# Two graph layers on one core: first sums of three chunks put ahead of the next logits, byte comparisons against a number held in PSUM, and destination one-hots moved to ScalarE

## What is computed

```python
def gat_conv(h, src, dst, fc_w, attn_l, attn_r, bias, heads, out_feats):
    feat = (h @ fc_w.T).reshape(n, heads, out_feats)
    el = jnp.sum(feat * attn_l, axis=-1)
    er = jnp.sum(feat * attn_r, axis=-1)
    e = jax.nn.leaky_relu(el[src] + er[dst], 0.2)
    m = jax.ops.segment_max(e, dst, num_segments=n)
    ex = jnp.exp(e - m[dst])
    ssum = jax.ops.segment_sum(ex, dst, num_segments=n)
    a = ex / ssum[dst]
    return jax.ops.segment_sum(feat[src] * a[..., None], dst, num_segments=n) + bias
```

## Time and profile before

| | us |
|---|---|
| median of three runs | 2154.1 |
| the profiled execution | 2160.66 |
| its span, first to last instruction | 2158.5 |
| first sums, gathers on POOL | 78 to 617 |
| second scores, VectorE's one-hots | 698.0 to 836.2 |
| gathers for the second sums, POOL | 693 to 1255 |
| mean granted TensorE clock | 0.80 |

### The profile page before, as it was taken

How to read it: one execution, slowest core, us unless ns; L and a number is a source line. 1 busy time by engine, 2 the same in 40 slices (tenths; PEclk the granted TensorE clock), 3 DMA queues, 4 the chain that set the end, 5 groups by cost and what they waited for, 6 DMA issues and landing times.

```text
span 2158.5 us, 28964 instructions
## 1 busy us (share of the span) xinstructions
PE 1510.8 (70%) x7753; PEld 1147.0 (53%) x7754; DVE 1450.5 (67%) x2290; ACT 419.1 (19%) x780; POOL 1369.4 (63%) x1396
## 2 busy tenths in 40 slices
PE   5345656666777443888566688877778777489997
PEld 3234544544666342676454545655555555368874
DVE  3457787777886786776444465777676666777766
ACT  1100000000004000000000043444444444110127
POOL 0477777777731888777777714677777777135544
PEclk9657877777888555999878788888787877689999
DMA  2654444444414664444434436899999999778811
GB/s 89 168 130 122 126 122 124 125 125 125 120 49 151 174 171 138 135 129 129 120 115 120 123 96 235 299 342 339 339 349 335 343 335 341 281 248 294 292 69 60
DMA packets 234909, 406.15 MB, mean 188 GB/s; under 512 B 33199, under 2 KB 171621, under 8 KB 228197
## 3 DMA queue, kind: packets, MB, share of 16 engines
q0 software_dynamic: 73216, 219.89, 32.7%
q1 hardware_dynamic: 161637, 185.66, 27.3%
HBM read 330.93 MB, written 74.48 MB: 188 GB/s over the span
## 4 chain that ended last, share of the span: by engine, by line
POOL 49%; PE 20%; issue 17%; DMA 7%; DVE 5%; SPq 1%; ACT 1%; ACTq 0%; DVEq 0%; POOLq 0%
POOL row_space L876 45%; PE ps L1190 9%; DMA row_space<-tab_kv,src_i 3%; DMA item_v<-row_space 3%; PE ps L1291 2%; PE ps L1412 2%; POOL base L885 2%; POOL acc L885 1%; PE ps L963 1%; PE ps L991 1%; PE ps L1300 1%; PE ps L1432 1%; POOL arena L885 1%; PE ps L1215 1%; DMA arena<-rows_block_dst 1%
## 5 line engine op out<-in xcount | busy, mean ns | idle before, releaser
L876 POOL DMA_INDIRECT row_space<-tab_feat,src_i x760 | 757.1, 996 | 302.7 <-issue 231.2
L876 POOL DMA_INDIRECT row_space<-tab_kv,src_i x416 | 394.2, 948 | 197.7 <-issue 123.7
L1190 PE MATMUL ps<-arena 128*128 128x257 f32 (+1 forms) x1664 | 422.0, 415 | 121.7 <-DVE arena L2170 115.6
L1190 PEld LDWEIGHTS ps<-arena 128*128 128x128 f32 x1664 | 339.6, 208 | 197.5 <-issue 139.0
L1291 PE MATMUL ps<-arena 128*128 128x265 f32 x768 | 234.8, 470 | 95.9 <-DVE ps L2413 47.3
L1086 PE MATMUL ps<-acc,arena 128*128 x832 | 284.3, 501 | 0.0
L2164 DVE TENSOR_TENSOR arena<-row_space,ps 128x1280 f32<-128x1280 f32 (+1 forms) x94 | 174.3, 1855 | 141.7 <-DMA row_space<-tab_feat,src_i 139.9
L1291 PEld LDWEIGHTS ps<-arena 128*128 128x128 f32 x768 | 177.1, 236 | 142.1 <-issue 102.8
L1582 ACT COPY acc<-ps 128x265 f32<-128x265 f32 (+2 forms) x75 | 28.3, 377 | 1105.6 <-PE ps L1190 545.1
L1982 DVE TENSOR_TENSOR arena<-row_space,ps 128x1024 f32<-128x1024 f32 x104 | 126.8, 1220 | 137.4 <-PE ps L1086 86.2
L1086 PEld LDWEIGHTS ps<-acc,arena 128*128 128x128 f32 x832 | 196.6, 248 | 38.3
(11 more groups left out here) (380 smaller groups left out, 2176.6 us busy)
## 6 DMA issues: line engine op xcount, KB each, us to landing
item_v<-row_space SPq DMA_DIRECT2D x52, 1024.0 KB, 7.9
row_space<-item_v SPq DMA_DIRECT2D x52, 1024.0 KB, 4.9
arena<-rows_block_dst SPq DMA_DIRECT2D x104, 128.0 KB
row_space<-tab_feat,src_i POOLq DMA_INDIRECT x760, 2.8
scores<-rows_block_dst SPq DMA_DIRECT2D x52, 128.0 KB
arena<-rows_src_low SPq DMA_DIRECT2D x52, 128.0 KB
row_space<-tab_kv,src_i POOLq DMA_INDIRECT x416
arena<-rows_type SPq DMA_DIRECT2D x52, 128.0 KB
```

What stands on the lines that cost most here:

```text
L876: nc.gpsimd.indirect_dma_start(rows_of_slot(s)[:, g, :], None, table, bass.IndirectOffsetOnAxis(ap=src_i[:, item:item + 1], axis=0),).then ...
L1190: last = nc.tensor.matmul(ps[:, SUM_BANKS:2 * SUM_BANKS][:, bass.ds(bs[g], 1), 0:width].rearrange("p a d -> p (a d)"), onehot[:, s % 2, g, ...
```

## The change

Three edits.

**First sums, order.** `sums_first` now runs chunks 9, 10 and 11, and `period` only chunks 0 to 8 and 12. Inside `sums_first` the terms of chunk c+2 are spread out: groups 0 and 1 between the builds, 2 and 3 between the steps of the softmax. On PE, register loads move behind `carries`, and each of these chunks has 11 warm products ahead of the shares and 6 behind the factors.

**Comparisons against PSUM.** ScalarE and VectorE write the partition's own number (and, for `hot`, the numbers 0 to 24) into spare columns of PSUM. The byte comparisons of the first sums, the sources' half of those of the second scores, and `hot` read that copy: `tensor_scalar` with a pointer becomes `tensor_tensor` with a broadcast column in PSUM.

**Second scores, destinations.** VectorE compares only the sources' row (1024 bytes instead of 2048). ScalarE makes the destinations' one-hots: Square of (byte - own number) into one of four buffers, then Relu of 1 - square. The broadcasts have four buffers instead of two; the sources' row waits for VectorE's one-hot, the destinations' row for ScalarE's Relu. PE waits for both one-hots.

```diff
+                def spread_both(u, s, first):
+                    for k, made in ((0, onehot_made), (1, dst_onehot_made)):
+                        if not first and k == 0:
+                            sp.wait_ge(made[s % 2], nth(u, s) + HALF)
+                        if not first and k == 1:
+                            sp.wait_ge(made[s % 2], nth(u, s) - 1)
+                        row = flat[k][bass.ds(u * (STEP * P // 2) + s * GROUP * P // 2, GROUP * P // 2)]
+                        sp.dma_start(bcast_words[:, s, k], row.partition_broadcast(P)).then_inc(bcast_in[s], 16)
...
                         pe.wait_ge(onehot_made[s % 2], nth(u, s) + (layer * HALF + 2))
+                        pe.wait_ge(dst_onehot_made[s % 2], nth(u, s) + 1)
...
-            idle("score2")
+            def dst_squares(u, s, first):
+                act.wait_ge(bcast_in[s], u * 32 + (32 + (broadcasts(1) if s < 2 else 0)))
+                if not first:
+                    act.wait_ge(dst_onehot_made[s % 2], nth(u, s) - 1)
+                nc.scalar.activation(dst_square[:, s], bcast[:, s, 1], ACT.Square,
+                                     bias=minus_part_no[:]).then_inc(act_step, 1)
+                step.add()
+            def dst_relu(u, s, still):
+                act.wait_ge(act_step, step.value() - still)
+                act.wait_ge(score_mm[s % 2], nth(u, s) + HALF)
+                nc.scalar.activation(onehot_t[:, s % 2, 1], dst_square[:, s], ACT.Relu, scale=-1.0,
+                                     bias=ones[:, 0:1]).then_inc(dst_onehot_made[s % 2], 1)
...
                 z = s % 2
-                dve.wait_ge(bcast_in[z], nth(u, s) * 32 + (32 + broadcasts(layer)))
-                vec.tensor_scalar(onehot_t[:, z], bcast[:, z], part_no[:], None,
+                dve.wait_ge(bcast_in[s], u * 32 + (32 + (broadcasts(layer) if s < 2 else 0)))
+                own = ps[:, 4 * z:4 * z + 1, NUMBERS_AT + BLOCKS:NUMBERS_AT + BLOCKS + 1].rearrange("p a x -> p (a x)")
+                vec.tensor_tensor(onehot_t[:, z, 0], bcast[:, s, 0], own.broadcast_to([P, GROUP * P]),
                                   ALU.is_equal).then_inc(onehot_made[z], 1)
...
-                    vec.tensor_scalar(dst_onehot[:, z], dst_bytes[:, z], part_no[:], None,
+                    vec.tensor_tensor(dst_onehot[:, z], dst_bytes[:, z], ps[:, SHARE_BANK, OWN_AT:OWN_AT + 1].broadcast_to([P, GROUP * P]),
                                       ALU.is_equal).then_inc(onehot_made[z], 1)
...
-                def sums_first(c, half, turn, last):
+                def sums_first(c, half, turn):
+                    terms, more, last = c + 2 < CHUNKS, c + 3 < CHUNKS, c == CHUNKS - 2
                     rescale(c)
                     for g in range(1, SLOTS):
                         build(c, half, g)
-                        if last and g < SLOTS - 1:
-                            next_terms(end, 0, g + 1, False)
+                        if terms and g < SLOTS - 1:
+                            next_terms(c + 2, half, g - 1)
...
-                    if CHUNKS - 4 < c < CHUNKS - 1:
-                        sums_first(c, c % 2, c // 2, c == CHUNKS - 2)
+                    if c < CHUNKS - 1:
+                        sums_first(c, c % 2, c // 2)
```

More of the change, by code:

```diff
@@ L386, in graph_layers @@
         slot_used = [sem(f"rows_used{s}") for s in range(2 * SLOTS)]
-        bcast_in = [sem(f"item_rows_broadcast{s}") for s in range(2)]
+        bcast_in = [sem(f"item_rows_broadcast{s}") for s in range(SLOTS)]
+        dst_onehot_made = [sem(f"destination_onehot_made{s}") for s in range(2)]
         onehot_made = [sem(f"onehot_made{s}") for s in range(2)]
@@ L501, in broadcasts @@
         def broadcasts(layer):
-            return 16 * HALF + 32 * HALF * (layer - 1) if layer else 0
+            return 16 * HALF + 32 * TURNS * (layer - 1) if layer else 0
         @block.sync
@@ L1300, in warm, with sums_first @@
                         nc.tensor.matmul(ps[:, TERM_BANK, 0:D], ident[:], w_b[:, 0, :], start=True, stop=True)
[L1302 to L1308, removed]
+                def sums_first(c, banks, cleared, pair):
+                    terms = c + 2 < CHUNKS
                     pe.wait_ge(sum_mm, c * CHUNK_COUNT + CREDIT)
@@ L1373, in chunk_sums @@
                 period(0, True, False, True)
-                with nc.tensor.Fori(0, CHUNKS - 4) as u:
+                with nc.tensor.Fori(0, CHUNKS - 5) as u:
                     period(u + 1, False, False, True)
-                sums_first(CHUNKS - 3, False)
-                sums_first(CHUNKS - 2, True)
-                warm(WARM_SUMS - 1)
-                period(CHUNKS - 1, False, True)
+                ahead = (*sum_banks(CHUNKS - 4, 0), term_blocks(CHUNKS - 2, 0))
+                for c in range(CHUNKS - 4, CHUNKS - 1):
+                    ahead = sums_first(c, *ahead)
+                period(CHUNKS - 1, False, True, known=ahead[0:2])
                 pe.wait_ge(sum_mm, QUADS + TICKS + CREDIT)
@@ L1609, in _, with dst_turn @@
             end()
-            idle("score2")
+            begin(act, "score2", ["dve", "pe"])
+            def dst_squares(u, s, first):
[10 more added lines that the diff above has]
+                                     bias=ones[:, 0:1]).then_inc(dst_onehot_made[s % 2], 1)
+            def dst_turn(u, first, last):
+                for s in range(SLOTS):
+                    dst_relu(u, s, 0 if last and s == SLOTS - 1 else 1)
+                    if not (last and s >= 2):
+                        dst_squares(u + (s + 2) // SLOTS, (s + 2) % SLOTS, first and s < 2)
+            dst_squares(0, 0, True)
+            dst_squares(0, 1, True)
+            dst_turn(0, True, False)
+            with nc.scalar.Fori(0, TURNS - 2) as u:
+                step.enter(u, SLOTS)
+                dst_turn(u + 1, False, False)
+                step.leave(TURNS - 2)
+            dst_turn(TURNS - 1, False, True)
+            for z in range(2):
+                act.wait_ge(dst_onehot_made[z], HALF)
+            end()
             soft(0, "soft2", H2, ITEMS // 4)
@@ L1887, in gat_scores @@
                 w = BLOCKS * heads
+                for z in range(2):
+                    then(vec.tensor_copy(ps[:, 4 * z, NUMBERS_AT:NUMBERS_AT + BLOCKS], iota_free[:, 0:BLOCKS]))
+                    then(vec.tensor_copy(ps[:, 4 * z, NUMBERS_AT + BLOCKS:NUMBERS_AT + BLOCKS + 1], part_no[:]))
                 el_v, er_v = er[:, :, 0:heads], er[:, :, heads:2 * heads]
```

85 lines of the change are left out of this document (49 added, 36 removed).

## The result

The kernel after takes 2129.05 us (median of 6 runs, 2123.95 to 2134.77), the kernel before beside it 2153.07 us (6 runs). The ratio is 0.989, interval 0.9866 to 0.9914: 24 us less. Measured a second time, beside some of the experiments, it was 2126.95 us, ratio 0.9901 (0.9886 to 0.9916). 2126 with a range of 2108 to 2146 had been predicted. The working of the second scores holds step by step; one term of the first sums is wrong, and an error of the other sign beside it hides this in the total.

What follows compares the result with a forecast made beforehand. It took POOL's gathers as the bound, with the wait for the second scores' end next. From the median 2154.1 us it took 7 (first sums) and 21 (second scores), 28 together, giving 2126 us; range 2108 to 2146.

Steps and rivals of the forecast that it cites:

- The term of 21 us: Second sums: gather group 17 starts 190 us after the first gather instead of 211; bounds 0 and 34 us.
- ScalarE's cover: Second scores: ScalarE's two instructions per group, 2.12 us, stay hidden only as long as ScalarE is not the bound.
- the forecast's loop: Second scores: four broadcast buffers, 5.0 us landing plus 4.24 us of ScalarE work, 2.31 us per group; 2.3 taken.
- A comparison with PSUM leaves gathers alone: Gathers beside comparisons with a PSUM operand keep their undisturbed pace, one per 1.25 us.
- (a): First sums: freed gathers, 0.155 us for each of 52 comparisons, about 8 us less until the last gather; bounds 0 and 17.8.
- (b): First sums: VectorE's comparison takes 0.48 us more, 1.9 us per chunk, hidden up to chunk 9 by the wait for gathers.
- (c): First sums, new order: VectorE's own work sets the end from chunk 9; logits of 12 at 613.5, 7 us less.
- PE waits that builds used to hide come in: First sums, from the rescale of chunk 9 to the logits of 12: 2 us more, bounds 0 and 6.
- Broadcasts did bind: Rival for the second scores: broadcasts bind harder, 2.6 us per group, scores end at 836, time 2141 us; chance 0.13.
- Gathers were freed: Answers the rival that byte comparisons with PSUM still stretch gathers and nothing is gained, 2154 us; chance 0.07.
- All of it: Rival: second scores at 2.12 us per group, first sums at their floor, 41 us less, 2113 us; chance 0.08.
- The slower case: Rival for the second scores: late broadcasts hold ScalarE's four buffers, 3.11 us per group, scores end 22 us later; chance 0.03.

Runs made afterwards that it cites:

- Experiment 9: Kernel before, two buffers, no ScalarE part; in the second scores VectorE compares both rows (2048 bytes) with the number in PSUM: 2182.6 us, ratio 1.0134.
- Experiment 8: Kernel after, with VectorE's 1024-byte comparison in the second scores put back to `tensor_scalar` with a pointer to `part_no`: 2125.93 us, ratio 0.9888.
- Experiment 7: Kernel after, order kept; in chunks 9 and 10 TensorE does term products of groups 0-2 before their sums, group 3's before lane ends: 2120.29 us, ratio 0.9852.

## Why the prediction was right and where it failed

**What bounds: right.** The second pass is bound by the later of two things, the gathers' pace and the scores' end. Experiment 9 frees the one and delays the other: its second pass is 588.0 us, 28 longer. Experiment 8 gives up part of the one and keeps the other: nothing is lost, since the slack covers it. No run shortens the scores with the gathers left at the pace of before, so that both are needed for the 21 us is shown from one side only.

**Second scores: right, and by its steps.** Comparison 1.22 us: 1.21. From a Relu's end to the Square in its buffer 5 us: 4.69 in the mean of 44 (4.06 to 5.74, from the start times in after). Pace 2.3: 2.33, and 2.28 from the fifth one-hot on. Scores' end 19 us earlier: from the first gather 125.8 us instead of 146.0, 20 earlier. Group 17 after 190 us: 188.7. POOL's wait 20: 18.15. The term of 21 us is 21.2 to 23.3 in the traces of after. Timed alone it was 16.8, at most 20.2; timed on top of the new comparison (0.9848 against 0.9956, measured apart) it was 23. ScalarE's cover was the tightest. From 700 to 800 us it is busy for 92.92 us and VectorE for 90.84; its pairs run back to back, 2.08 us per group, where no broadcast is late, and the late ones add 7.1 us. Together with experiment 8, where a shorter VectorE hardly helped, this points at ScalarE and its broadcasts as what holds the pace now, as the forecast's loop had it. No run shortens ScalarE's part, so this is argued and not shown.

**A comparison with PSUM leaves gathers alone: right.** No row of before had bytes and PSUM together; beside such comparisons a gather takes 0.948 us in experiment 9. The Trainium skill, page "SBUF — State Buffer", section "Who interferes with whom", distinguishes between `tensor_scalar`, which can enter a two-port mode, and an instruction with one SBUF input outside it; the traces agree: 0.28 us more per comparison in experiment 8, nothing in experiment 9.

**First sums, (a) and (b): right in kind, (a) too small.** 8 us had been taken for the freed gathers, the traces show 10 to 13 (536.4 against 523.6 to 526.8). The gather of the earlier trace rows is 0.25 us too long (1.20 instead of 0.95), but no run shows the 0.155 us per comparison of this term. What the trace of before shows, when each of the 52 comparisons is laid over the gathers that it overlaps (0.948 us is undisturbed), is 0 to 0.52 us, 0.19 in the mean and 9.9 in all; the 52 of after add nothing. The comparison's 0.46 us more (0.745 to 1.208) is hidden but for some 2 us at most.

**First sums, (c): wrong, and this is the step that failed.** The logits of 12 came at 613.34 where 613.5 stood in the forecast, but not by its terms: 4.4 us of it are the earlier start of the profiled execution. From the rescale of chunk 9 to these logits the forecast had 613.5 - 524.3 = 89.2 us; it was 96.6. Term by term, against the 91.2 of before: the wait for gathers, -5.4, came true. VectorE's work, +2.9 forecast, grew from 73.64 to 76.82 us, +3.2. "PE waits that builds used to hide come in, such as 2.34, I take 2 (bounds 0 and 6)" is the term that fails. The waits for term products grew from 5.4 to 15.9 us, +10.5; first before, then after (in total, times, longest):

```profile
DVE scores L2286 <- PE ps L1235: 4.4, 2, 2.5
DVE scores L2286 <- PE ps L1244: 1.0, 1, 1.0
```
```profile
DVE scores L2346 <- PE ps L1252: 11.0, 4, 3.8
DVE scores L2346 <- PE ps L1261: 4.9, 2, 2.6
```

Other waits for TensorE fell by some 3 us, the rest of the sum. I had looked at VectorE's queue alone, which the builds fill, and not at what stands ahead of the term products in TensorE's: 16 sums, 6.81 us of them where TensorE had been idle. Experiment 7 moves just these products and the stretch falls to 88.5 us, near the forecast's 89.2. So the new order was priced as if the products were there when VectorE asks.

Hence the split of the sum was wrong as well: "without (a) nothing" for the order (it is +7.5 us alone, +9 in the finished kernel), and the comparison by itself is worth more (9.5 us) than comparison and order together (1.5 us timed alone; 4.6 in the trace of after). 2126 was met because the second scores carry nearly all of it, and because the larger (a) paid for the order. For the first sums that is luck: 7 us were forecast, and 1.5 (4.1 at most) were there.

**Rivals.** Broadcasts did bind a little (7.1 us of waits within the scores) but far from 2.6 per group. Gathers were freed. "All of it" (2113) assumed the first sums at their floor, which the order prevented, and 2.12 us per group, where 2.33 was measured; with the order out or mended, 2118 to 2122 us come nearer to it. The slower case stayed away: 2.33 per group against 3.11.

**Open.** Why the order alone costs 7.5 us in time where its trace shows 1.4 to 2.9, and why the second scores alone gain 16.8 us in time where their stage shows 21.8. Whether a further step brings the kernel below 2118 us was not tried: the next wait is POOL's 18 us for the slot of group 6.

## What to carry to other kernels

When work is moved ahead on one engine, read the queue of the engine that feeds it: a small product behind sixteen large ones is as late as they are, and moving it ahead of them gave some 10 us back here (0.9901 to 0.9852, measured apart). When two limits set one end, ask for each how much slack the other leaves: the freed gathers with longer scores lost 29 us, and gathers slower by 14 us lost nothing that could be measured while POOL had 18 us to wait. Measure the parts of a change one by one, since a sum that comes out right can hide a part that costs.

## What the runs showed of the hardware that was not expected

- A comparison of bytes against a broadcast PSUM column takes 1.21 us for 1024 columns and 2.29 us for 2048; with a pointer in SBUF it is 0.744 and 1.31. In experiment 9 this makes 52 comparisons 51 us longer (68.0 to 118.8 us busy), and the scores end 30 us later.
- The pointer form stretches gathers by 0.28 us per comparison of 0.744 us (experiment 8), while it is itself hardly held up: 742 to 865 ns.
- How much one such comparison costs a gather goes by when it starts. In the first sums of before, the 11 that start 0.06 to 0.09 us into a gather cost nothing, and the 8 that start between two gathers cost the next one most, 0.32 to 0.52 us.
- After a pause of 5.6 us 16 sum products took 6.81 us at a granted clock of 0.55, the next 16 3.83 us at 1.00.
